# Moving one small subtraction ahead of a long scan in VectorE's order (macaron block, one Trainium2 core)

## The reference

```python
x = x + 0.5 * ffn(layernorm(x), ...)
x = x + attn(layernorm(x), ...)
x = x + 0.5 * ffn(layernorm(x), ...)
```

```python
lr = xf @ m1                                                  # 256 -> 64
mask_logits = jnp.einsum('bl,lxy->bxy', lr, m2) + mb          # 16 groups of 64
quant_mask = jnp.argmax(mask_logits, axis=-1)
w = w1p[j, quant_mask]
mid = jnp.einsum('ai,aji->aj', xf, w)
v = w2p[j, quant_mask]
res = jnp.einsum('ai,aij->aj', jax.nn.relu(mid), v) + b2
```

## Time and profile before

| | |
|---|---|
| median of 3 runs | 3441.06 us (3439.2 to 3452.6) |
| the profiled execution's own time | 3442.63 us |
| its span | 3440.7 us |
| first x_out of the first FFN stage, last one | 56.3 us, 989.4 us |
| first x_out of the second FFN stage, last one | 2504.9 us, 3438.1 us |
| TensorE busy | 3238.1 us (94%) |
| VectorE busy | 2946.1 us (86%) |
| ScalarE, GpSimd busy | 1744.2 us (51%), 1525.9 us (44%) |
| granted TensorE clock, mean | 0.989 |

### The profile page before, as it was taken

One profiled execution on the slowest core, in us unless ns is written; L12 is line 12 of the kernel. 1 busy time (PEld: TensorE's weight loads), 2 busy tenths in 40 slices (PEclk: granted clock), 3 DMA queues, 4 the chain that ended last, 5 costly groups with the idle time before them and its releaser, 6 DMA issues. The chain is left out here.

```text
span 3440.7 us, 98135 instructions
## 1 busy us (share of the span) xinstructions
PE 3238.1 (94%) x35456; PEld 2676.2 (78%) x35456; DVE 2946.1 (86%) x5231; ACT 1744.2 (51%) x4040; POOL 1525.9 (44%) x2298
## 2 busy tenths in 40 slices
PE   5999999999979999999999999999699999999999
PEld 4888888888866766777677667777588888888888
DVE  7999999999968888888888888888599999999998
ACT  3333333333337777777777777777433333333332
POOL 3333333333325656665666666666333333333332
PEclk9999999999999999999999999999799999999999
DMA  3111111111111111111111111111111111111111
GB/s 84 56 52 53 55 50 55 52 53 55 51 35 34 33 37 34 35 34 35 37 34 35 37 32 37 37 32 37 33 52 54 55 50 55 52 53 55 50 55 45
DMA packets 169664, 156.26 MB, mean 45 GB/s; under 512 B 19316, under 2 KB 169204, under 8 KB 169592
## 3 DMA queue, kind: packets, MB, share of 16 engines
q1 hardware_dynamic: 169592, 155.27, 15.0%
HBM read 104.86 MB, written 50.33 MB: 45 GB/s over the span
## 5 line engine op out<-in xcount | busy, mean ns | idle before, releaser
L568 PE MATMUL mid_ps<-xT_hl,w_hl 128*128 128x128 f16 x12288 | 729.5, 219 | 0.0
L415 PE MATMUL res_ps<-w_hl,midT_hl 128*128 128x256 f16 x6144 | 712.5, 273 | 1.2 <-DVE x_out L536 1.2
L372 POOL TENSOR_TENSOR var_eps<-moments,eps_col 128x1 f32<-128x1 f32 x384 | 111.5, 290 | 1344.5 <-DVE moments L368 1344.5
L568 PEld LDWEIGHTS mid_ps<-xT_hl,w_hl 128*128 128x128 f16 x12288 | 698.8, 98 | 0.5
L415 PEld LDWEIGHTS res_ps<-w_hl,midT_hl 128*128 128x128 f16 x6144 | 589.5, 98 | 65.8 <-DVE midT_hl L523 1.7
L476 ACT ACTIVATE midT_hl<-mid_ps 128x1024 f16<-128x1024 f32 x256 | 262.2, 1024 | 695.4 <-PE mid_ps L579 695.4
L502 DVE TENSOR_TENSOR_SCAN runmax<-restart,logits_ps 128x1024 f32<-128x1024 f32 x256 | 581.1, 2270 | 3.8 <-PE logits_ps L557 3.7
L387 ACT ACTIVATE xn_hl<-xc,rstd 128x256 f16<-128x256 f32 x384 | 197.3, 514 | 433.9 <-POOL rstd L377 353.4
L523 DVE SCALAR_TENSOR_TENSOR midT_hl<-mid_ps,midT_hl 128x1024 f16<-128x1024 f32 x256 | 313.3, 1224 | 15.4 <-ACT midT_hl L476 7.5
L507 DVE TENSOR_TENSOR step<-runmax 128x1024 bf16<-128x1024 f32 x256 | 314.8, 1230 | 8.0
L377 POOL TENSOR_TENSOR rstd<-var_eps,minus_half 128x1 f32<-128x1 f32 x384 | 292.9, 763 | 34.5 <-POOL var_eps L372 8.9
(11 more groups left out here) (148 smaller groups left out, 6716.2 us busy)
## 6 DMA issues: line engine op xcount, KB each, us to landing
x<-x_out SPq DMA_DIRECT2D x256, 128.0 KB, 1.7
x_in<-x SPq DMA_DIRECT2D x256, 128.0 KB, 2.0
x_res<-x SPq DMA_DIRECT2D x256, 128.0 KB, 2.1
x_in<-in_L_attn_x SPq DMA_DIRECT2D x128, 128.0 KB, 2.0
x_res<-in_L_attn_x SPq DMA_DIRECT2D x128, 128.0 KB, 2.1
out<-x_out SPq DMA_DIRECT2D x128, 128.0 KB, 2.0
w_f<-in_L_ffn_w SPq DMA_DIRECT2D x1, 1024.0 KB, 7.9
w_f<-in_L_ffn_w SPq DMA_DIRECT2D x2, 512.0 KB, 10.6
```

The source lines that it names most:

```text
L415: last = nc.tensor.matmul(dst, left(lp, k), right(rp, k), start=(k == 0 and lp == rp), stop=(k == blocks - 1 and lp == 1))
L568: nc.tensor.matmul(mid_ps[t.slot][:, cols], w1_hl[:, wp, k, cols], xT_hl[:, t.ring, xp, k], start=(c % PER_BANK == 0 and k == 0 and wp == xp),
```

## The change

In the list of VectorE's stages in the FFN, `low_low` with offset 2 stands ahead of `first_max` with offset 1, where it stood between `first_max` and `reached`. Nothing else differs: the same instructions run with the same semaphores and the same operands. VectorE's order in step s becomes finish(s-2), stats(s+5), low_low(s+2), first_max(s+1), reached(s+1), aggregate(s+5), low(s+4), reject(s+1), mid_low(s).

```diff
-                    pipeline(dve, [(finish, -2), (lambda t: norm.stats(dve, t), 5),
-                                   (first_max, 1), (low_low, 2), (reached, 1),
+                    pipeline(dve, [(finish, -2), (lambda t: norm.stats(dve, t), 5), (low_low, 2),
+                                   (first_max, 1), (reached, 1),
                                    (lambda t: norm.aggregate(dve, t), 5), (lambda t: norm.low(dve, t), 4),
                                    (reject, 1), (mid_low, 0)],
                              tiles, base, UNROLL, LONGEST_LAG)
```

## The result

The changed kernel takes 3474.59 us (median of 6 runs, 3470.29 to 3480.05), the kernel before in the same comparison 3442.81 us (6 runs). The ratio is 1.009, 95% interval 1.008 to 1.010: slower by 0.9%, where 3470 was forecast. The profiled execution took 3472.19 us, with a span of 3470.3.

A forecast was written before the change was run, and what follows sets the result against it. It took a closed loop through VectorE and GpSimd, 7.41 us a step, as the bound. Gaps adding 0.115 us in each of 240 steps make 28 us; from the median, 3441.06, that is 3469, said as 3470, range 3455 to 3491.

The forecast's parts named there:

- The bound: FFN steady steps: a closed loop through VectorE and GpSimd sets the step, mean 7.41 us, in 240 steps.
- The three gaps: On VectorE, stats to low_low, low_low to scan, scan to reached: each +0.03 us, sum +0.09 against -0.02 before.
- the one ahead of mid_low: VectorE's gap from reject to mid_low: would go from +0.03 to -0.08 us, giving nothing back.
- The sum: VectorE's gaps between stats and aggregate added up: 0.115 us more per step, 28 us over 240 steps.
- rival "no change": On VectorE, a semaphore or another order costs nothing, so the loop stays as long, 3441 us; chance 0.08.
- The size: The loop in each FFN step gets 0.115 us longer, 28 us over 240 steps.
- The last hand-over: GpSimd to finish: 0.21 us in 42 of 120 steps, else 0.09; a shift could give 3459 to 3489 us.
- low_low's new wait: low_low waiting for ScalarE's copy: some 0.1 us in the first steps, gone in a step or two, costed at nothing.
- TensorE at the transposes: TensorE's 0.23 us wait per step ahead of the transposes, in step with low_low, would go; gain costed at nothing.
- TensorE's busy share: TensorE in the FFN stages: its busy share would fall; no size given.
- GpSimd's 2.58 as fixed: GpSimd's chain from centre to add_bias in the loop was taken to stay 2.58 us long.

The follow-up runs named there:

- e3: The changed kernel with GpSimd's two stages swapped, add_bias ahead of centre: 3385.04 us, ratio 0.9850 to the kernel before.
- e4: The kernel before with GpSimd's two stages swapped, add_bias ahead of centre: 3381.80 us, ratio 0.9845 to the kernel before.
- e6: The kernel before with low_low on partitions 0 to 63 and add_bias ahead of centre on GpSimd: 3382.23 us, ratio 0.9818.
- e7: The changed kernel with one more 128x1 addition on GpSimd ahead of each add_bias: 3513.96 us, ratio 1.0208 to the kernel before.
- e1: The changed kernel with low_low on partitions 0 to 63, waiting for ScalarE's second copy: 3408.24 us, ratio 0.9918 to the kernel before.
- e2: The kernel before, in its own order, with low_low on partitions 0 to 63: 3440.54 us, ratio 1.0012 to the kernel before.
- e5: The kernel before with low_low on partitions 0 to 63, and reached also waiting for the low_low just ahead: 3426.10 us, ratio 0.9952.
- e8: The changed kernel with add_bias ahead of centre and one more 128x1 GpSimd addition ahead of add_bias: 3388.59 us, ratio 0.9843.

## Why the prediction was right

- **The bound.** Right: the loop finish, scan, aggregate, GpSimd's four operations, finish. It closes in both traces, e3, e4 and e6 cut it, and e7 lengthens it by what was put in.
- **The three gaps.** Right, each +0.03. e1 shows that the ones on both sides of low_low come from its partitions. The Trainium skill's rule on starting quadrants (VectorE: DVE Perf Modes, "Two Vector instructions with no wait between them") agrees with every gap of the steady steps that is no wait, also with the one ahead of mid_low, which went to -0.08 as forecast and gave nothing back.
- **Which gap the change added.** The sum had all three, but not this reading of them. The loop had two held starts before the change (low_low and `reached`) and has two after it (low_low and the scan). What is new is that `reached` comes directly behind the scan that it waits for: +0.03 there in the changed kernel and in e1, -0.08 in e2 with low_low between. e5 shows it on another pair: a wait for the instruction directly in front moved the gap from -0.08 to +0.10. So the rival "no change" was wrong where it took a semaphore between VectorE's own instructions to be free.
- **The size.** The forecast took 0.115 a step, measured were 0.135. 0.017 of the difference is the scan's own duration (2.270 to 2.287 us, median), which the sum took as fixed. The scan is recorded longer wherever it starts behind the end of the instruction in front, whether held (2.287) or waiting for TensorE (2.287 in e4); where it overlaps that end it has 2.27 (before, e1, e2, e5). Against that, the shorter last steps of each stage, 4.6 us, weren't in the sum. The two misses nearly cancelled, and that was luck.
- **The last hand-over.** 42 of 120 steps stayed the long kind in both stages, so that term moved nothing.
- **low_low's new wait.** Right in the changed kernel's steady steps: no idle time ahead of low_low. Wrong for the first ones, where the forecast had 0.1 us, gone in a step or two: in the first four tiles of the first stage low_low waited 1.0, 1.8, 1.4 and 0.3 us for ScalarE (before, only for the first tile, 1.2). The first x_out comes 1.1 us later (57.4 against 56.3). In e3, where TensorE is the bound, it stays at 0.43 us.
- **TensorE at the transposes.** Wrong in what would be seen. I wrote that TensorE would no longer stand ahead of the transposes in step with low_low. It still does, 0.32 behind low_low's end: 413.09 + 0.29 = 413.38, and 413.70 in the weight loads:

```profile
413.70 0.24 PEld L402 LDWEIGHTS front_ps<-ident,xn_hl 128*128 128x128 f16 x4 [0.32 <-issue]
```

  It ran ahead of VectorE until the first thing it needs from it in a step stopped it, and after the change that is low_low again. The 0.32 is the median in both kernels. Less the wait, TensorE's step is the same in both, 7.41 - 0.23 = 7.18 and 7.55 - 0.36 = 7.18: slack of TensorE shows up as a wait somewhere as long as another loop sets the step. The removal of this wait was what the change was for, and the wait grew from 0.23 to 0.36. Right was that TensorE's busy share would fall: 194.2 of the 200 us from 400 to 600, against 197.6 before.
- **GpSimd's 2.58 as fixed.** Right here, and named as an assumption. e2 shows how near it stood to another value, 2.85 to 2.93.

## What to carry to other kernels

A stall on the busiest engine isn't the bound if that engine has slack; look for the closed loop whose parts add up to the step, hand-overs included, and test it by adding a small operation of known length. In such a loop the order of VectorE's instructions has a price: here 0.11 us for each start that couldn't overlap the end of the one before. Two things did that in this kernel. One is an operand that starts at partition 64, twice in the loop in either order. The other is a wait for the result of the instruction directly in front; that one the change brought in, and with another instruction in between the same wait cost nothing. And before moving things inside a loop, see whether it can be cut: swapping two GpSimd stages was worth 1.5%, where the best run that left them as they were (e1) gained 0.8%.

## What the runs showed of the hardware

GpSimd's small operations end 0.05 us behind a VectorE operation with two SBUF inputs: var_eps behind `low` in the kernels before and after (median 0.049 and 0.048 us over 60 steps), and behind `reject` in e2 (0.053). The Trainium skill (SBUF — State Buffer, "Who interferes with whom") says that such an instruction and a GpSimd one that reads SBUF shut each other out for a whole instruction; the trace agrees. A GpSimd addition of the same size takes 0.19 us in e7, where it runs beside mid_low, which has one SBUF input. What I had not expected is who gets in when `low` ends with `reject` right behind it. With the same spacing of starts on VectorE (`low` to `reject` 0.37 in all of them), GpSimd got in wherever `reached` had started behind the end of the instruction in front, held (before, e4) or waiting for it (after, e1, e3, e5, e7, e8). It never got in where every start since the scan had overlapped (e2, e6): 0.34 against 0.96 us for the same addition. What decides it inside is open; the runs show only which order has which outcome.
